# Cross-attention in a one-core decoder layer: rows of maxima sent ahead of the stores of normalised rows, and the routed tile placed ahead of a maximum

## What is computed

```python
x = x + attn(layernorm(x))          # 32 heads, 8 kv heads, rope, causal, sinks
x = x + xattn(layernorm(x), ctx, ctx)
x = x + ffn(layernorm(x))           # one of 8 experts by router, plus a shared expert

# xattn(q, k, v), b = 64, d = 64, m = 256: 8 heads of 8 tokens each,
# the 256 features are the queries and the keys
qh, kh, vh = (a.reshape(b * 8, d // 8, -1) for a in (q, k, v))
qk = einsum('bdm,bdn->bmn', qh, kh) / sqrt(d // 8)
ret = einsum('bmn,bcn->bcm', softmax(qk), vh)

# router
logits = x @ router_w.T
top_vals, top_idx = top_k(logits, 1)
xr = x[None] * sigmoid(scores).T[:, :, None]
```

## Time and profile before

| | us |
|---|---|
| median of 3 runs | 2088.55 |
| lowest, highest | 2078.5, 2088.84 |
| profiled execution | 2081.61 |
| its span (first to last instruction) | 2079.7 |
| PE busy | 1882.5 (91%) |
| DVE busy | 1136.2 (55%) |
| ACT busy | 801.4 (39%) |
| POOL busy | 607.2 (29%) |

### The profile page before, as it was taken

One profiled execution on the slowest core, in us unless ns is written; L12 is line 12 of the kernel. 1 busy time (PEld: TensorE's weight loads), 2 busy tenths in 40 slices (PEclk: granted clock), 3 DMA queues, 4 the chain that ended last, 5 costly groups with the idle time before them and its releaser, 6 DMA issues. The chain is left out here.

```text
span 2079.7 us, 45535 instructions
## 1 busy us (share of the span) xinstructions
PE 1882.5 (91%) x15632; PEld 1433.1 (69%) x15633; DVE 1136.2 (55%) x2205; ACT 801.4 (39%) x1495; POOL 607.2 (29%) x1120
## 2 busy tenths in 40 slices
PE   3999999999999999999779899899997599999997
PEld 2778778778777778778657676666675355666665
DVE  5665665665665665665467676667674222222221
ACT  3333333333333333333336666666665111111111
POOL 2222322322322322321223333333333210024443
PEclk9999999999999999999979999999999699999999
DMA  5011111111111111111133433433341173222221
GB/s 167 27 40 44 45 38 44 44 38 46 42 38 49 40 38 50 38 38 47 41 100 98 104 105 102 106 101 108 102 115 57 52 272 105 70 64 67 66 65 40
DMA packets 142008, 148.34 MB, mean 71 GB/s; under 512 B 26962, under 2 KB 136598, under 8 KB 140154
## 3 DMA queue, kind: packets, MB, share of 16 engines
q1 hardware_dynamic: 136186, 133.46, 22.8%
q0 software_dynamic: 5760, 14.06, 2.2%
HBM read 93.46 MB, written 54.11 MB: 71 GB/s over the span
## 5 line engine op out<-in xcount | busy, mean ns | idle before, releaser
L1119 DVE TENSOR_REDUCE xmax<-bankX 128x4 f32<-128x1024 f32 x256 | 310.1, 1217 | 149.7 <-PE bankX L1204 149.2
L1074 ACT ACTIVATE xe<-bankXT 128x512 f32<-128x512 f32 x512 | 293.4, 597 | 125.0 <-PE bankXT L1215 110.2
L1215 PE MATMUL bankXT<-stq,stk 98*128 98x256 f32 x1024 | 233.6, 315 | 34.9 <-DMA stq<-sh 28.7
L543 DVE TENSOR_TENSOR oTl<-bankV,oTh 128x512 fp32r<-128x512 f32 x128 | 88.6, 692 | 304.9 <-ACT oTh L431 304.9
L1215 PEld LDWEIGHTS bankXT<-stq,stk 98*128 98x128 f32 x1024 | 160.9, 197 | 73.4 <-ACT xe L1074 48.6
L1204 PE MATMUL bankX<-stk,stq 96*128 96x256 f32 x1024 | 177.2, 299 | 13.7 <-DMA rw<-in_rw 11.1
L649 PE MATMUL bankQ<-wqh,xnTh 128*128 128x512 f32 x384 | 189.1, 493 | 0.0
L1530 DVE TENSOR_TENSOR hid<-bankU,gate 128x512 f32<-128x512 f32 x72 | 49.8, 692 | 246.3 <-PE bankU L1583 243.1
L1476 ACT ACTIVATE gate<-bankG 128x512 f32<-128x512 f32 x72 | 43.0, 597 | 347.6 <-PE bankG L1583 347.6
L360 POOL TENSOR_TENSOR prob<-prob,rden 128x1024 f32<-128x1024 f32 x64 | 121.9, 1905 | 170.8 <-DVE rden L539 170.8
L1204 PEld LDWEIGHTS bankX<-stk,stq 96*128 96x128 f32 x1024 | 151.4, 204 | 16.3 <-DMA rw<-in_rw 11.3
(11 more groups left out here) (176 smaller groups left out, 3862.9 us busy)
## 6 DMA issues: line engine op xcount, KB each, us to landing
stackk_d<-chl SPq DMA_DIRECT2D x96, 128.0 KB, 2.3
stackq_d<-q2hl SPq DMA_DIRECT2D x96, 128.0 KB, 2.3
stk<-stackk_d SPq DMA_DIRECT2D x32, 384.0 KB
stq<-stackq_d SPq DMA_DIRECT2D x128, 96.0 KB
wexp<-in_wexp SPq DMA_DIRECT2D x8, 1536.0 KB, 8.3
x_d<-x SPq DMA_DIRECT2D x64, 128.0 KB, 1.8
xrden<-inv_d SPq DMA_DIRECT2D x64, 128.0 KB, 2.5
xin<-xg_d SPq DMA_DIRECT2D x40, 128.5 KB, 2.1
```

The costliest lines, as they stand in the source:

```text
L543: nc.vector.tensor_tensor(oTl[g % 2][:], bV[:, 0, :].rearrange("p (a b) -> p a b", a=4), oTh[g % 2][:].bitcast(F32), ALU.subtract).then_in ...
L1074: nc.scalar.activation(xe[q][:].rearrange("p n m -> p (n m)"), bT[:, q % 2, :], ACT.Exp).then_inc(s_xe, 1)
L1119: nc.vector.tensor_reduce(xmax[tile[1] % 2][:, :, a:b + 1:b - a].rearrange("p m h -> p h m"), bS[:, 2 * (pr % 2):2 * (pr % 2) + 2, :].rear ...
L1215: ins = nc.tensor.matmul(bT[:, q % 2, n * D:(n + 1) * D], stk[p][0:98, hd // 4, n * P:(n + 1) * P], stq[p][0:98, hd, :], start=True, stop= ...
```

## The change

On SP the block with the two stores moves from behind `inverses_out` to behind `inverses_in`, so that the rows of maxima are sent right behind the reciprocals. On DVE `place` moves from behind `max_x` of slot 6 to ahead of it.

```diff
                 if four:
                     inverses_out(z)
-                if five:
-                    yp = y[1] % 2
-                    sp.wait_ge(s_norm, at(y) + 1)
-                    sp.dma_start(G.xn3_d[bass.ds(at(y) * P, P), :], xn3[yp][:]).then_inc(s_fst[yp], 16)
-                    sp.dma_start(G.x2_d[bass.ds(at(y) * P, P), :], x2[yp][:]).then_inc(s_fst[yp], 16)
                 if two:
                     w = prev(tile, 1)
                     sp.wait_ge(s_shv, at(w) + 1)
...
                 if four:
                     inverses_in(z)
+                if five:
+                    yp = y[1] % 2
+                    sp.wait_ge(s_norm, at(y) + 1)
+                    sp.dma_start(G.xn3_d[bass.ds(at(y) * P, P), :], xn3[yp][:]).then_inc(s_fst[yp], 16)
+                    sp.dma_start(G.x2_d[bass.ds(at(y) * P, P), :], x2[yp][:]).then_inc(s_fst[yp], 16)
                 if one:
                     need(sp, s_cTp, t - 1)
...
                 for r in range(STEPS):
+                    if five and r == 6:
+                        place(y, routing)
                     if one:
                         max_x(tile, r)
...
                     if five and r == 4:
                         choose(y, routing)
-                    if five and r == 6:
-                        place(y, routing)
                     if four and r == 7:
                         stats_of(z)
```

## The result

| | before | changed |
|---|---|---|
| median, us (4 runs each) | 2084.18 | 2018.74 |
| lowest, highest | 2078.5, 2088.84 | 2016.39, 2022.56 |
| profiled execution, its span | 2081.61, 2079.7 | 2022.56, 2020.7 |

The changed kernel takes 0.969 of the time, 95% interval 0.966 to 0.972. The kernel before varies by 10 to 20 us from one execution to the next; in four later jobs, of 9 to 13 runs each, its median was 2078.7 to 2082.2. Its 2084.2 here, the median of four runs, is the highest of the five, so the gain of 65 us may be 2 to 5 us too large.

The account below looks back on a forecast made before the run. PE, busy 91% of the span, was taken as the bound, with time to win only where it idles or runs slowly. 26 (maxima) + 8 (`place`) + 22 (clock) = 56 us took 2081.6 to 2025.6, median 2028; range 2014 to 2058.

Parts of the forecast that it names:

- Part 1 at 26 us: SP queue: sending the rows of maxima ahead of the stores removes PE's wait for them, 26 us; bounds 15 and 26.3.
- The clock at 22 us: PE, 28 steps: without the wait for the maxima, 22 of 24 us lost to slow clock return; bounds 0 and 25.
- The rival in which the falls stay: PE clock: falls remain, the two moves alone give 34 us, 2047.6 or up to 2054 us; chance 0.14.
- Part 2 at 8 us: DVE: `place` ahead of slot 6's maximum ends PE's 16.3 us wait for `posx`, of which 8 us becomes time.
- If PE comes 0.54 us earlier, ACT can follow by 0.29 only: ACT's exponentials: nearly gapless, so only 0.29 us per step was counted as gained, 28 x 0.29 = 8 us.
- The bound of 16.3 us: PE at `turn_ctx`: upper bound if the whole wait for `posx` became time, 16.3 us; lower bound 0.
- a slightly larger wait of PE or PEld for `xe`: Profile sign of a right forecast: PE or PEld would wait slightly longer for the exponentials; PEld waited 41.4 us before.
- The rival of late loads: SP queue: stores right before the next tile's loads delay them, possibly slower than before, 2095 us at 9.5 us needed; chance 0.06.
- these keep their place: SP queue: the next tile's loads are not issued later, since the sum of SP's issues is the same.
- The sum: 28 steps: 26 + 8 + 22 = 56 us off 477.5, a step becoming 15.05 us; profiled execution 2025.6, median 2028.

Follow-up runs that it names:

- e1: Kernel before with only the rows of maxima sent ahead of the stores, `place` left behind slot 6's maximum: 2029.8 us, ratio 0.975.
- e3: Changed kernel with the two stores moved to the end of SP's step, behind the loads: 2012.9 us, ratio 0.967; 2011.2 us when run again.
- e4: Changed kernel with the next tile's five loads moved to the head of SP's step: 2011.1 us, ratio 0.966; 2009.7 us when run again.
- e8: e4 with `place` put back behind slot 6's maximum, as in the kernel before: 2025.0 us, ratio 0.974.
- e6: e4 with `place` moved behind slot 7's maximum, so that PE waits longer for `posx`: 2099.8 us.
- e5: e4 with the rows of maxima sent behind `inverses_in`, so that PE waits for them again: 2162.9 us.
- e2: Kernel before with only `place` moved ahead of slot 6's maximum, stores still ahead of the rows of maxima: 2076.6 us, ratio 0.9985.
- e7: Changed kernel with both edits, loads at the head of SP's step and stores at its end: 2027.2 us, ratio 0.973.

## Why the prediction was right

The time, 2018.7, lies in the range of 2014 to 2058 and 9 us below the predicted 2028; the direction and the mechanism hold. The parts are less exact than the sum: part 2 gave more than forecast, the clock a little less, the loads took some back, and 8 us of the span came from outside the 28 steps.

- *Part 1 at 26 us.* The wait for the maxima went from 26.3 to 0.8. Right, and e1 shows that it needs no help from part 2, which the prediction wanted for the longest waits.
- *The clock at 22 us.* Busy time fell by 18.8 us in the changed kernel, 20.7 with part 1 alone, 25 to 26 where hardly anything waits (e3, e4: 431.0 to 405.1 and 405.6). The mechanism is now shown: waits of 1.8 us at one place and 2.8 us at another, put in, bring the falls back, and with them gone there is no fall in the 28 steps. The rival in which the falls stay got 0.14 and did not come. The rule of the Trainium skill named there ("A second HAM failure mode: psum-queue depth-cycling" in "TensorE: Matmul & The Clock Gate") that frequent micro-idles suffice is not borne out for the small ones: in e8 the waits of 0.6 us, and 90 short waits of the weight loads for exponentials, left the clock at 2.4 GHz.
- *Part 2 at 8 us.* The step that was off, by size: "If PE comes 0.54 us earlier, ACT can follow by 0.29 only". The bound of 16.3 us was nearer: e8 against e4 gives 14 to 16. The prediction looked at ACT's gaps alone. The copy of the maxima in the step of the earlier trace rows is this row of the timeline of before:

```profile
1414.02 0.36 ACT L1054 ACTIVATE sh<-bankM 32x256 fp32r<-32x256 f32 x1
```

  From the first of ACT's exponentials of that stretch to this copy it took 1414.02 - 1408.38 = 5.64 us before and takes 1471.08 - 1465.83 = 5.25 now. That is the 0.29 and 0.1 more. Where ACT's pressure went is in the lists of waits of e8 and e4: without the waits for `posx` (16.6 us in e8's 28 steps), PEld waits 31.8 us for exponentials instead of 20.9, but PE's own idle time fell by 11.5 us all the same and its busy time by 2.1. So ACT did push back, as the prediction said, by some 11 us on the weight loads, and most of that lay beside running products. An engine without gaps is a bound only where its lateness reaches the idle time of the engine that waits for it. The sign named for this, "a slightly larger wait of PE or PEld for `xe`", came out the other way in the total (41.4 to 26.6), because part 1 alone lowers it to 19.9.
- *The loads.* The rival of late loads was priced as "it just fits", with 6.9 us needed of 7.0, and given 0.06 as an all-or-nothing case. It came as a part: 7 waits, 7.0 us, and the two low stretches of the clock. In the good step the scores start at 1483.22, 6.9 us behind the loads' issue at 1476.36, which is just the 6.9 of the prediction's sum; in the late one they start at 1422.89, 7.3 us behind the issue at 1415.55. e3 and e4 price the late loads at 7 to 8 us in the time. The argument "these keep their place" failed here: stores and maxima change sides, and the loads went out only 0.5 us sooner behind the reciprocals while the step got some 2 us shorter. The Trainium skill's rule named there, that a DMA engine consumes the descriptors of one issuer's ring in their order ("DMA: Bandwidth & Descriptors", "Queues, rings and completion order"), fits: with the stores not ahead, in either way, the queries come in time. The runs would look the same if only SP's issue of the stores counted, so they don't show the rule by itself.
- *The sum.* Forecast for the 28 steps 477.5 - 56 = 421.5 us, measured 426.5: the late loads and their falls, less what part 2 gave more. That the total is still better than forecast is in part luck. The 8 us from outside these steps were in no term of the sum, and 3.5 of them are chance; they outweigh the 5 us missing inside, so the profiled execution, 2022.6, is 3 us below its forecast of 2025.6. The other 6 us are the median, placed 2.4 us above the profiled execution because the 2088.6 of three runs of before was on the high side; it came 3.8 below.

## What to carry to other kernels

Where the trace shows TensorE waiting about a microsecond once in each round and the granted clock falling behind it, count the wait at about twice its length: here 26 us of waits carried 20 to 25 us of slow clock with them, 50 us carried 42 (e6, busy time against e4), 80 carried 66 (e5), and 24.5 carried 33 (e2, against e3). A single such wait may cost nothing more. But a second, smaller wait removed alone can be worth nothing, since the falls can then come more often (e2); take away the wait that stands ahead of the falls first.

When small, urgent DMAs and large ones share one queue, order the queue by when each is needed: what is urgent goes first, what nobody waits for goes last, and the step after the change needs its own check for what is late next, since every other deadline in it has moved closer.

## What the runs showed of the hardware that was not expected

- Taking 15 us of idle out of a 477 us stretch made TensorE's clock worse: 0.92 instead of 0.95 on average, with single stretches of 13.7 us at 1.2 GHz in which PE was busy throughout, behind a wait of only 1.29 us (e2).
- Waits of 0.6 us, once a step, left the clock at 2.4 GHz over 429 us (e8); waits of 1.8 us at the same place brought it down in nearly every step (e6). Length alone does not decide: a wait of 0.70 us in the kernel before had a fall behind it, one of 1.86 us in the changed kernel had none.
- Loads first and stores last each gave some 8 us; together they lost 8 us against the changed kernel (e7), where the landing of the two 16 KB DMAs went from 2.2 to 2.4 us in the median, behind 1 MB of transfers; the longest, 3.3 us, is no longer than in the other versions.
